# A graph layer's adjacency product on one core: column groups two and three read as rows of 2440 columns for the first 16 of 39 row slots

## The reference, cut to what matters

```python
h = jnp.maximum(_layernorm(x, axis=-1), 0.0)          # x: (5000, 64)
neighbors = adj_matrix @ h                            # adj: (5000, 5000)
neighbors = neighbors / (num_neighbors[:, None] + EPS)
self_and_neighbor = jnp.concatenate([h, neighbors], axis=-1)
out = self_and_neighbor @ fc_w.T + fc_b               # fc_w: (64, 128)
x = x + jax.nn.relu(out)
```

## Time and profile before

| | |
|---|---|
| median of 3 runs | 246.71 us (246.56 to 246.78) |
| the profiled execution | 246.56 us |
| its span, first to last instruction | 245.1 us |
| TensorE busy | 204.6 us, 83% |
| VectorE busy | 41.3 us, 17% |
| ScalarE busy | 15.2 us, 6% |
| moved by DMA | 102.79 MB, mean 419 GB/s |

### The profile page before, as it was taken

One profiled execution on the slowest core, in us unless ns is written; L12 is line 12 of the kernel. 1 busy time (PEld: TensorE's weight loads), 2 busy tenths in 40 slices (PEclk: granted clock), 3 DMA queues, 4 the chain that ended last, 5 costly groups with the idle time before them and its releaser, 6 DMA issues.

```text
span 245.1 us, 2433 instructions
## 1 busy us (share of the span) xinstructions
PE 204.6 (83%) x1084; PEld 85.5 (35%) x1084; DVE 41.3 (17%) x101; ACT 15.2 (6%) x35; POOL 4.3 (2%) x14
## 2 busy tenths in 40 slices
PE   0268989797869786998799999999896699798995
PEld 0143334242325232453244333333232233133663
DVE  1762033304300200050000440221000000002301
ACT  2130021201200110010000210000000000000000
POOL 6000000000000000000000000000000000000000
PEclk9997999999999999999799999999999999999999
DMA  8899999999999999999999999999999999999996
GB/s 297 377 435 441 455 431 430 428 428 429 426 430 424 448 431 428 428 428 409 414 443 433 433 443 405 430 439 433 425 433 439 409 428 428 413 419 420 420 401 266
DMA packets 7109, 102.79 MB, mean 419 GB/s; under 512 B 1364, under 2 KB 2172, under 8 KB 3900
## 3 DMA queue, kind: packets, MB, share of 16 engines
q1 hardware_dynamic: 6400, 102.37, 98.3%
q10 hardware_dynamic: 700, 0.28, 0.4%
HBM read 101.37 MB, written 1.28 MB: 419 GB/s over the span
## 4 chain that ended last, share of the span: by engine, by line
DMA 65%; PE 18%; issue 12%; DVE 2%; SPq 2%; DVEq 0%
DMA raw<-adj_group 65%; PE acc L605 16%; DVE rnn_diag L458 2%; PE turned L605 1%; SPq L246 1%; PE y L595 1%; SPq L259 1%; SPq L250 0%; PE y L587 0%; PE turned L558 0%; DVE out_sb L521 0%; DVE rnn_diag L466 0%; PE acc L653 0%; DVE rnn_diag L463 0%; SPq L255 0%
## 5 line engine op out<-in xcount | busy, mean ns | idle before, releaser
L605 PE MATMUL acc<-raw,g_sb 128*64 128x512 f32 (+1 forms) x780 | 159.1, 562 | 24.1 <-DMA raw<-adj_group 24.1
L605 PEld LDWEIGHTS acc<-raw,g_sb 128*64 128x64 f32 x780 | 56.1, 139 | 121.9 <-issue 85.9
L605 PE MATMUL turned<-raw,g_sb 128*64 128x196 f32 x156 | 15.1, 336 | 1.4 <-DMA raw<-adj_group 1.1
L487 DVE TENSOR_TENSOR sums<-acc,rnn_bc 128x512 f32<-128x512 f32 x4 | 2.6, 686 | 59.6 <-PE acc L605 57.6
L570 PE MATMUL y<-w_both,ht 128*128 128x256 f32 (+1 forms) x40 | 11.9, 437 | 0.8 <-ACT ht L344 0.8
L437 DVE TENSOR_TENSOR out_sb<-y,bias 128x128 f32<-128x128 f32 x20 | 4.4, 284 | 47.9 <-ACT g_sb L350 47.9
L605 PEld LDWEIGHTS turned<-raw,g_sb 128*64 128x64 f32 x156 | 10.2, 136 | 6.4 <-DMA raw<-adj_group 4.6
L570 PEld LDWEIGHTS y<-w_both,ht 128*128 128x128 f32 x40 | 8.0, 217 | 3.9 <-issue 2.7
L558 PE MATMUL turned<-ident,h_pairs 128*128 128x128 f32 x20 | 3.7, 315 | 4.7 <-DVE h_pairs L425 4.7
L413 DVE TENSOR_REDUCE var<-sums 128x8 f32<-128x512 f32 x5 | 3.4, 686 | 23.3 <-ACT sums L324 23.3
L513 DVE TENSOR_TENSOR out_sb<-y,out_sb 128x512 f32<-128x512 f32 (+1 forms) x5 | 3.2, 639 | 22.2 <-PE y L637 19.0
(11 more groups left out here) (57 smaller groups left out, 44.9 us busy)
## 6 DMA issues: line engine op xcount, KB each, us to landing
raw<-adj_group SPq DMA_DIRECT2D x9, 5120.0 KB, 27.3
raw<-adj_group SPq DMA_DIRECT2D x7, 4096.0 KB, 26.3
raw<-adj_group SPq DMA_DIRECT2D x4, 2048.0 KB, 29.2
raw<-adj_group SPq DMA_DIRECT2D x7, 784.0 KB, 24.8
raw<-adj_group SPq DMA_DIRECT2D x1, 3840.0 KB, 24.5
raw<-adj_group SPq DMA_DIRECT2D x3, 1024.0 KB, 26.7
raw<-adj_group SPq DMA_DIRECT2D x4, 392.0 KB, 20.2
x_sb<-x SPq DMA_DIRECT2D x2, 576.0 KB, 4.9
```

What stands on the lines that cost most here:

```text
L605: last = nc.tensor.matmul(acc[b][s * HALF:(s + 1) * HALF, 0:width], g_sb[:, t, :], raw[:, c + c0:c + c0 + width], start=g < G - 1 and t == ...
```

## The change

There are four groups of loads in place of three. Slots 0 to 15 of the former groups 1 and 2 come from one array of 2440 columns (2048 + 392), so a load of four slots brings 9760 columns a lane and its slots are multiplied into banks 3, 4 and 5 at once. Then slots 16 to 38 of the 2048 columns, then slots 16 to 38 of the 392 columns, in arrays of their own as before. `RUNS` gives each group its runs. Of each run's pieces none changes. The ring for the wide rows has 12 slots of 2440 columns (three loads), where the one for 2048 columns had 16 (four loads). The remainder of all 2440 columns is done in one call after slot 15 of the wide rows, where before there were two calls; the buffer, memset and semaphore of the second go. The flips of banks 0 to 2 stand one slot earlier; flips 3 and 4 stand after slots 25 and 29 of the last group.

```diff
--- before.py
+++ after.py
@@ -26,15 +26,18 @@
 
 
 
+
+
 P = 512
-GROUPS = [(0, 5, 0), (5, 4, 3), (9, 1, 5)]
+GROUPS = [(0, 5, 0), (5, 5, 3), (5, 4, 3), (9, 1, 5)]
+RUNS = [(0, 10), (0, 4), (4, 10), (4, 10)]
 ALIGN = 1
 
 BANK_BLOCKS = (0, 2, 4, 5, 7, 9)
 
 
-STEPS = [(4, 4, 4, 4, 4, 4, 4, 4, 4, 4), (4, 4, 4, 4, 4, 4, 4, 2, 2, 1), (4, 4, 4, 4, 4, 4, 4, 2, 2, 1)]
-RING = [(12, 0), (16, 4), (82, 62)]
+STEPS = [(4, 4, 4, 4, 4, 4, 4, 4, 4, 4), (4, 4, 4, 4), (0, 0, 0, 0, 4, 4, 4, 2, 2, 1), (0, 0, 0, 0, 4, 4, 4, 2, 2, 1)]
+RING = [(12, 0), (12, 4), (16, 12), (82, 5)]
 
 
 def gnn_layer(nc, x, adj_groups, num_neighbors, fc_t, fc_b, out):
@@ -70,7 +73,8 @@
     WIDEST = max(WIDTH) // BLOCK
 
     def banks(g):
-        return range(GROUPS[g][2], GROUPS[g + 1][2] if g + 1 < G else LAST + 1)
+        first, n, b = GROUPS[g]
+        return range(b, BANK_BLOCKS.index(first + n) if first + n < BANK_BLOCKS[-1] + 1 else LAST + 1)
 
     def sides(g, b):
 
@@ -81,7 +85,7 @@
 
     LOADS = []
     for g in range(G):
-        for m in range(FULL + 1):
+        for m in range(*RUNS[g]):
             n = RUN if m < FULL else TAIL_RUN
             LOADS += [(g, m, i, min(n, i + STEPS[g][m])) for i in range(0, n, STEPS[g][m])]
     FIRST_LOAD = [[ld[0] for ld in LOADS].index(g) for g in range(G)]
@@ -105,12 +109,12 @@
     TURN_AFTER = {(0, 3): 1, (0, 7): 2, (0, 13): 3, (0, 21): 4}
     WEIGH_AFTER = {(0, 5): 1, (0, 11): 2, (0, 19): 3, (0, 27): 4}
     SPREAD_AFTER = (0, 38)
-    REM_AFTER = {(0, 33): 0, (1, 15): 1, (1, 23): 2}
-    FLIP_AFTER = {(1, 7): 0, (1, 9): 1, (1, 11): 2, (2, 9): 3, (2, 13): 4}
-    PRELOAD_AFTER = (1, 19)
+    REM_AFTER = {(0, 33): 0, (1, 15): 1}
+    FLIP_AFTER = {(1, 6): 0, (1, 8): 1, (1, 10): 2, (3, 25): 3, (3, 29): 4}
+    PRELOAD_AFTER = (2, 19)
     LN_OPS = 8
 
-    REM_LOADS = [sum(1 + (w % (2 * BLOCK) > 0) for w in WIDTH[:g + 1]) for g in range(G - 1)]
+    REM_LOADS = [sum(1 + (w % (2 * BLOCK) > 0) for w in WIDTH[:g + 1]) for g in range(2)]
 
     with ExitStack() as ctx:
         def sb(name, shape, dt=F32):
@@ -126,8 +130,6 @@
         g_sb = sb("g_sb", [LANES, TILES, F])
         cen = sb("cen", [LANES, BT * F])
         h_pairs = [sb(f"h_pairs{i}", [LANES, BT * F]) for i in range(2)]
-
-        adj_rem_last = h_pairs[1]
         ht = [sb(f"ht{i}", [LANES, BLOCK]) for i in range(2)]
         ht_rows = sb("ht_rows", [LANES, 2 * SIDE])
         ht_rem = sb("ht_rem", [LANES, LANES])
@@ -167,7 +169,6 @@
         bias_copied = sem("bias_copied")
         landed = [sem(f"landed{k}") for k in range(LANDINGS)]
         rem_loaded = sem("rem_loaded")
-        rem_last_loaded = sem("rem_last_loaded")
         ln_dve = sem("ln_dve")
         ln_act = sem("ln_act")
         ident_cleared = sem("ident_cleared")
@@ -282,8 +283,6 @@
                 k = slice(s * HALF, (s + 1) * HALF)
                 nc.gpsimd.memset(own_half[k, k], 1.0).then_inc(ones_ready, 1)
             pool.wait_ge(ones_ready, 3)
-            pool.wait_ge(turned_done, SETS - 1)
-            nc.gpsimd.memset(adj_rem_last[:], 0.0).then_inc(rem_cleared, 1)
 
         def scalar_program(act):
             def load_rem(g):
@@ -298,12 +297,8 @@
                 act.dma_start(adj_rem[lanes, 0:k, 0:BLOCK],
                               rows[:, 0:k * BLOCK].rearrange("r (k c) -> r k c", k=k)).then_inc(rem_loaded, 16)
                 if w > k * BLOCK:
-                    act.dma_start(halves(adj_rem[lanes, k, :])[:, :, 0:BLOCK // 2],
+                    act.dma_start(halves(adj_rem[lanes, k, :])[:, :, 0:(w - k * BLOCK) // 2],
                                   rows[:, k * BLOCK:w].rearrange("r (s c) -> r s c", s=2)).then_inc(rem_loaded, 16)
-                if g == 1:
-                    act.wait_ge(rem_cleared, 3)
-                    act.dma_start(halves(adj_rem_last[lanes, :])[:, :, 0:SIDE],
-                                  adj_groups[G - 1][REM0:N, :].rearrange("r (s c) -> r s c", s=2)).then_inc(rem_last_loaded, 16)
 
             def load_few():
 
@@ -537,7 +532,7 @@
             add_bias(4)
             for b in range(SETS):
                 expand(b)
-            for g in range(G - 1):
+            for g in (0, 2):
                 for b in banks(g):
                     if b == ALONE:
                         scale_alone(g)
@@ -603,26 +598,21 @@
                 for b in banks(g):
                     for s, c0, width in sides(g, b):
                         last = nc.tensor.matmul(acc[b][s * HALF:(s + 1) * HALF, 0:width], g_sb[:, t, :],
-                                                raw[:, c + c0:c + c0 + width], start=g < G - 1 and t == 0, stop=t == CH - 1,
+                                                raw[:, c + c0:c + c0 + width], start=t == 0, stop=t == CH - 1,
                                                 tile_position=(0, s * HALF))
                 if i == i1 - 1:
                     last.then_inc(load_used, 1)
 
             def remainder(g):
-
-                if g < G - 1:
-                    pe.wait_ge(rem_loaded, 16 * REM_LOADS[g])
-                else:
-                    pe.wait_ge(rem_last_loaded, 16)
+                pe.wait_ge(rem_loaded, 16 * REM_LOADS[g])
                 for b in banks(g):
                     for s, c0, width in sides(g, b):
                         if width == BLOCK:
                             k = adj_rem[:, c0 // BLOCK, 0:BLOCK]
                         else:
-                            k = adj_rem[:, (c0 - s * width) // BLOCK, :] if b == ALONE else adj_rem_last[:]
-                            k = halves(k)[:, s, 0:width]
+                            k = halves(adj_rem[:, (c0 - s * width) // BLOCK, :])[:, s, 0:width]
                         last = nc.tensor.matmul(acc[b][s * HALF:(s + 1) * HALF, 0:width], g_sb[:, CH, :], k,
-                                                start=g == G - 1, stop=False, tile_position=(0, s * HALF))
+                                                start=False, stop=False, tile_position=(0, s * HALF))
                 last.then_inc(rem_used, 1)
 
             def flip(b):
```

## The result

The changed kernel takes 247.12 us (median of 20 runs, 246.86 to 247.41), the kernel before 246.78 (20 runs, 246.45 to 246.91). The ratio is 1.0015, 95% interval 1.0009 to 1.0020: 0.34 us slower. The forecast was 247.2. The profiled execution has a span of 245.7 us, where the one before had 245.1.

The account below looks back on a forecast made before the run. The prediction took the stream of `adj` loads on the DMA engines as the floor. Its terms, +0.67 for the flips and -0.19 for the stream, gave +0.48 us on the median of 246.71, so 247.2 us, range 246.4 to 247.8.

Parts of the forecast that it names:

- The end: Last stage on 392 columns: two flips with only 9 slots after them show as +0.67 us of their 1.17.
- The stream: `adj` loads: four loads fewer at 0.048 us each save 0.19 us, with bounds of +0.46 and -0.52.
- The ring: Three places for wide loads where four were: 10.7 us of cover, so SP does not stop; no cost.
- PE's work, remainder, flips 0 to 2, DVE: Same PE work, merged remainder and moved flips where PE waits for loads, DVE's scaling of banks 3 and 4: no cost.
- The store: 1152 KB store near the end: issued about 240.8, done about 244.3, clear of the last store by 0.3 us; no cost.
- Rivals 1 and 3: Wide rows slow the stream, +0.46, 247.8 us, chance 0.09; flips don't show, 246.5 to 246.2 us, chance 0.14.
- rival 2: The big store becomes the last thing or mixes with the last store: some 0.5 us, 247.7, chance 0.07.
- rival 5: Ring starves the stream or PE idles more; excluded as far as 10.7 us of cover go, no chance of its own.
- Rival 4: Small 784 KB loads cost more, 2.0 us each: four wide loads save 0.57, time 246.8, chance 0.05.
- The signs: Trace marks: wide loads 11.5 to 11.7 us apart, unbroken 18 x 2 PE rows, `scale_last` 0.5 us later, store near 240.6.

Follow-up runs that it names:

- run 1: Changed kernel with flips 3 and 4 after slots 19 and 23 instead of 25 and 29: 246.43 us, ratio 0.9990 to the kernel before.
- run 3: Kernel before, narrow loads throughout, with flips 3 and 4 after slots 25 and 29 instead of 9 and 13: 247.36 us, ratio 1.0026.
- run 2: Changed kernel with flip 3 after slot 19 instead of 25, flip 4 still after 29: 246.36 us, ratio 0.9987 to the kernel before.
- Run 7: Changed kernel with flips after 19 and 23 and two ring places for wide loads, not three: 252.70 us, ratio 1.0232 to the kernel before.
- Run 4: Changed kernel with flips 3 and 4 after slots 27 and 31 instead of 25 and 29: 247.49 us, ratio 1.0031 to the kernel before.
- run 6: Changed kernel with flips after 19 and 23, four wide loads cut to sixteen of one slot: 247.39 us, ratio 1.0026 to the kernel before.
- run 5: Kernel before with every load of the 392-column group cut to one slot, 25 more loads: 248.54 us, ratio 1.0072.
- run 9: Changed kernel with flips after 19 and 23, each load issued as two, even and odd lanes: 246.49 us, ratio 0.9992 to the kernel before.

## Why the prediction was right, step by step

The forecast was +0.48 us on the kernel before, and +0.34 was measured (0.22 to 0.49 by the interval). That 247.12 lies nearer still to the 247.2 is in part luck: the kernel before had a median of 246.78 this time, not the 246.71 that I counted from.

- **The end.** Forecast +0.67 us, by carrying the row of before over slot by slot. TensorE was to end at 242.50; DVE starts at 242.51. Undoing it gives 0.6 (run 1), doing it alone in the old kernel gives 0.64 (run 3), and in both late kernels the stretch from the last wait to DVE's start grew by 0.65. The non-linear part, that 0.67 is what is left of 1.17, is shown by run 2.
- **The stream.** Forecast -0.19 us, 0.048 for each load saved. This term was too small. Measured are -0.25 (run 1) and -0.27 (from run 3 to the changed kernel), each give or take some 0.25; by 9 ns a lane piece, 8 pieces an engine and four loads fewer it is 4 x 8 x 0.009 = 0.29. With it the sum is 0.67 - 0.29 = +0.38. The line through two landing distances could not find so small a term: 0.02 us more in the distance of 1.90 turns 0.048 into 0.07, and in run 3's trace single distances of these loads run from 1.88 to 1.95. Its bounds, +0.46 and -0.52, held it.
- **The ring.** No hole, as forecast. Run 7 shows that the three places matter, and that one of the reasons had escaped me.
- **PE's work, remainder, flips 0 to 2, DVE.** No cost showed; these were not tried one by one, but the terms of the two steps above add up to +0.38 where +0.34 was measured, with an error of some 0.14, so nothing points to a cost of theirs.
- **The store.** Forecast issued at 240.8, done at about 244.3 and clear of the last one by 0.3 us; it was issued at 240.81, ended at 244.3, and the last store's data began at about 244.65. The 0.7 us from issue to data was misread from the earlier trace rows: the data of the last store moves from 244.0, so it is 0.8, for both stores alike, and the margin stays. Run 4 shows the rival at two slots further on.
- **Rivals 1 and 3** are excluded by runs 1 to 3, **rival 2** by the 3.2 us behind DVE's start, **rival 5** by the DMA row. **Rival 4**, small loads that cost more, was right in kind but not in size: 0.07 us a load, for my 0.048 and its own 0.14. The 2 us that I had estimated for the four loads from the Trainium skill's table ("DMA: Bandwidth & Descriptors", section Bandwidth) are far from the 0.25 and 0.27 measured.
- **The signs.** One unbroken run of 36 rows, 3.21 us long, the big store at 240.81 and the wide loads 11.70 and 11.68 us apart came as named. DVE started 0.63 us later, not 0.5, because this execution had lost 0.20 us ahead of the change, about what the stream gained behind it.

## What to carry to other kernels

Where a stream of loads bounds a kernel, look for the last load that the computing engine still waits for: what the engine does behind it is on the path. Work placed earlier is hidden, as long as it is smaller than the slack that the engine has over all the loads that still follow. Moving a piece of work within the same stage by a few loads can outweigh what larger transfers save. Price small transfers that are queued one behind the other by their contiguous pieces, not by their number, and when a ring gets fewer places, follow it past its end into the loads that reuse its space.

## What the runs showed of the hardware that I had not expected

- Two transfers of 64 lanes each, lanes 0 to 63 and 64 to 127 in turn, stream at 207 GB/s with all 16 engines busy; the same with even and odd lanes at 430. The Trainium skill ("SBUF — State Buffer", section "Door 1: The DMA port swizzle") says that one bit of the lane's number, the one worth 64, selects between the two ports of a cluster, so that lanes 0 to 63 reach half of the ports. The two windows agree with it: half the rate where a transfer stays on one side of that bit, the full rate where it has lanes on both.
- In the run at half rate TensorE's granted clock was 0.76 on average from 60 to 200 us, with TensorE busy for 75.8 of 140 us; at full rate it was 0.98.
- A contiguous piece of a lane costs about 9 ns of its DMA engine beside its bytes, at 9760 bytes a piece (run 6) as at 1568 (run 5), and a transfer itself nothing that shows when others are queued, about 0.01 us at most (run 9).
- A small store issued behind a large one on another queue began to move data only when the large one was done, in the one trace that has the case (run 4): issued at 243.52, data from about 244.8, the large one done at 244.6. In five traces without the large one in the way it took 0.8 us from issue to data. Which step makes it wait is open.
